# Three edits to the six-layer stage of a one-core transformer kernel: order on TensorE and GpSimd, and a loop written out

## The reference, cut to what matters

```python
q, k, v = split(shift_tokens(x) @ Wqkv)          # 16 heads of 64
q, k = l2norm(q) * qs, l2norm(k) * ksc
q = q * cos * scale + rotate_half(q) * sin * scale
k = k * cos * inv + rotate_half(k) * sin * inv
# windows of 32 tokens, each looks at itself and the one before
attn = softmax(where(mask, -big, q @ k.T * 8.0))
x = (attn @ v) @ Wo + x
x = ffn_layer(shift_tokens(x), ...) + x
```

## Time and profile before

| | |
|---|---|
| median of 3 runs | 2736.19 us (2731.33 to 2745.01) |
| the profiled execution | 2730.72 us |
| its span in the trace | 2728.9 us |
| granted TensorE clock, mean | 0.912 |
| busy: TensorE, VectorE, ScalarE, GpSimd | 2169.6, 1973.4, 1509.5, 1492.2 us |

### The profile page before, as it was taken

How to read it: one execution, slowest core, us unless ns; L and a number is a source line. 1 busy time by engine, 2 the same in 40 slices (tenths; PEclk the granted TensorE clock), 3 DMA queues, 4 the chain that set the end, 5 groups by cost and what they waited for, 6 DMA issues and landing times.

```text
span 2728.9 us, 53797 instructions
## 1 busy us (share of the span) xinstructions
PE 2169.6 (80%) x21684; PEld 1154.6 (42%) x21780; DVE 1973.4 (72%) x2087; ACT 1509.5 (55%) x1863; POOL 1492.2 (55%) x1031
## 2 busy tenths in 40 slices
PE   4768875888998989888889889889988756678734
PEld 1111123555555555555555555555555411111334
DVE  1766628888888888888888888888889426676211
ACT  2255564566676666666766676666766321455600
POOL 5500017777776776777776777777777234100033
PEclk7787897999999999999999999999999866897967
DMA  4100000000001000100010000000000001000133
GB/s 149 60 19 25 13 2 1 17 2 17 2 2 26 17 2 2 26 2 17 1 26 2 17 2 9 19 17 2 1 9 2 1 18 67 22 27 13 32 92 86
DMA packets 55828, 59.08 MB, mean 22 GB/s; under 512 B 13142, under 2 KB 45012, under 8 KB 55508
## 3 DMA queue, kind: packets, MB, share of 16 engines
q1 hardware_dynamic: 53444, 50.77, 6.1%
q0 software_dynamic: 2128, 4.72, 0.7%
HBM read 44.07 MB, written 11.01 MB: 20 GB/s over the span
## 4 chain that ended last, share of the span: by engine, by line
PE 36%; POOL 19%; DVE 17%; issue 16%; ACT 9%; DMA 2%; SPq 1%; POOLq 0%; DVEq 0%; ACTq 0%
PE bank L735 5%; PE bank L706 4%; PE bank L859 4%; DVE big L1463 4%; PE bank L923 4%; PE bank L933 4%; POOL big L580 3%; POOL big L597 3%; POOL big L581 3%; DVE big L1569 3%; POOL small L590 2%; ACT big L1180 2%; ACT pxs L1305 2%; PE bank L976 2%; DVE small L1563 2%
## 5 line engine op out<-in xcount | busy, mean ns | idle before, releaser
L1463 DVE TENSOR_REDUCE big<-bank 128x1 f32<-128x512 f32 x512 | 327.7, 685 | 199.3 <-PE bank L706 195.3
L602 POOL TENSOR_TENSOR sc<-sc,small 128x1024 f32<-128x1024 f32 x96 | 263.4, 2744 | 365.4 <-DVE small L1605 365.4
L859 PE MATMUL bank<-wqk,xs 128*128 128x512 f32 x768 | 359.2, 610 | 13.6 <-ACT xs L1261 8.3
L933 PE MATMUL bank<-pxs,mw 128*128 128x256 f32 x1536 | 366.2, 382 | 0.0
L1296 ACT ACTIVATE sc<-sc 128x1024 f32<-128x1024 f32 x96 | 101.5, 1057 | 464.0 <-DVE sc L1595 463.9
L933 PEld LDWEIGHTS bank<-pxs,mw 128*128 128x128 f32 x1536 | 291.1, 192 | 102.7 <-issue 71.9
L1180 ACT ACTIVATE big<-bank 128x1024 f32<-128x1024 f32 x256 | 250.2, 1026 | 140.1 <-PE bank L720 137.1
L1569 DVE TENSOR_TENSOR big<-big,rotCl 128x2048 f32<-128x2048 f32 x96 | 226.2, 2356 | 78.1 <-POOL big L581 78.1
L706 PE MATMUL bank<-pxs 48*128 48x512 bf16 x512 | 183.6, 439 | 117.1 <-DVE big L1463 74.0
L1563 DVE TENSOR_REDUCE small<-big 128x32 f32<-128x2048 f32 x96 | 219.0, 2281 | 39.5 <-ACT big L1274 30.2
L1584 DVE TENSOR_TENSOR big<-big,small 128x1024 f32<-128x1024 f32 x192 | 246.5, 1284 | 1.1 <-POOL small L592 1.1
(11 more groups left out here) (244 smaller groups left out, 3945.1 us busy)
## 6 DMA issues: line engine op xcount, KB each, us to landing
wqk<-in_L_ffn_Wqkv SPq DMA_DIRECT2D x12, 512.0 KB, 4.4
pxs<-part_rows SPq DMA_DIRECT2D x64, 96.0 KB
pxs<-part_rows SPq DMA_DIRECT2D x64, 64.0 KB
wqk<-in_L_ffn_w SPq DMA_DIRECT2D x16, 256.0 KB, 3.0
wvt<-in_wv_layers_t SPq DMA_DIRECT2D x6, 512.0 KB, 4.7
wol<-in_L_ffn_Wo SPq DMA_DIRECT2D x6, 512.0 KB, 5.8
part_rows<-big SPq DMA_DIRECT2D x24, 128.0 KB
part_rows<-sc SPq DMA_DIRECT2D x24, 128.0 KB
```

The source lines that it names most:

```text
L602: pool.tensor_tensor(p3, p3, rden(i).unsqueeze(2).broadcast_to([P, LH, 64]), ALU.mult).then_inc(l_pn, 1)
L859: m = pe.matmul(bank[:, 2 - 2 * half + c, :], xs[:, b % 2, WIN + i * P:WIN + (i + 1) * P], wqk[:, (2 * half + c) * 512:(2 * half + c + 1) ...
L933: m = pe.matmul(bank[:, 6, part * 2 * P:(part + 1) * 2 * P], mw[:, 2 * (a % 4) + s, a // 4, :], pxs[:, part, a, s, :], start=(a == 0 and s ...
L1463: dve.tensor_reduce(nm[:, qt, 2 * p + r:2 * p + r + 1], bank[:, 4 + r, :], AX.X, ALU.max, negate=True).then_inc(a_mx, 1)
```

## The change

On TensorE, `turn_windows(T)` moves from the end of the slot to the place behind the projections, ahead of the second half of mixing and of `weigh(T - 1)`. Its wait becomes the softmax subtraction of T (`l_e`), since bank 4 holds the scores until then; `weigh` now waits for the eviction of the turned tile (`l_xe`), and the scores for the first eviction of `weighed(T - 2)` (`l_pc`). ScalarE evicts the turned tile right behind the exponentials. GpSimd does the half rotations of T+2 ahead of the division of T. `layer_slots`, and with it the slots of all engines, and SyncE's loop become Python loops, so all rounds stand in the program, with constants to wait on.

```diff
@@ layer_slots
-            with eng.Fori(0, DEPTH - 1) as l:
+            for l in range(DEPTH - 1):
                 for j in range(2, 2 + BATCH):
@@ sync
-            with sp.Fori(1, DEPTH) as l:
+            for l in range(1, DEPTH):
                 load_layer(l, False)
@@ gpsimd slot
-                normalise(T, i)
                 if ahead >= 2:
                     if b == BATCH - 1 and i == 2:
                         pool.wait_ge(l_tab, 3 * l + 6)
                         settle(pool)
                     turn_swapped(T + 2, (i + 2) % TILES)
+                normalise(T, i)
@@ tensor
             def scores(T, it, i):
-                if not (isinstance(T, int) and T == 0):
-                    pe.wait_ge(l_xe, T)
+                if not (isinstance(T, int) and T < 2):
+                    pe.wait_ge(l_pc, 2 * T - 3)
+                elif T == 1:
+                    pe.wait_ge(l_xe, 1)
+                settle(pe)
@@
             def turn_windows(T, b, i):
-                if isinstance(T, int) and T == 0:
-                    pe.wait_ge(l_e, 1)
-                else:
-                    pe.wait_ge(l_pc, 2 * T - 1)
+                pe.wait_ge(l_e, T + 1)
+                settle(pe)
@@ tensor slot
                         project(...)
+                turn_windows(T, b, i)
                 if feeds:
                     feed(fed, fl, i, 2)
                 if mixes:
                     mixing(it, l, b, i, 1)
                 if not (first and i == 0):
                     pe.wait_ge(l_pt, T)
-                    pe.wait_ge(l_e, T + 1)
+                    pe.wait_ge(l_xe, T + 1)
@@
                     weigh(T - 1, i + 3)
                 if feeds:
                     feed(fed, fl, i, 3)
-                turn_windows(T, b, i)
@@ scalar slot
                 exponentials(T, i)
+                windows(T, i)
                 if ahead >= 2:
                     take(T + 2, i % 2, 0)
@@
                         weighed(T - 1, it if i else it - 1, (i - 1) % TILES, half)
-                windows(T, i)
```

## The result

The changed kernel takes 2819.5 us (median of 4 runs, 2811.4 to 2822.3), the one before 2733.8 us in the same comparison: a ratio of 1.0304, 95% interval 1.027 to 1.0338. It is slower, as forecast (2771), but by 86 us instead of 35, and lies above the range (2718 to 2812).

The account below looks back on a forecast made before the run. A ring of waits between GpSimd and VectorE, 17.06 us a turn, with no engine full, was taken as the bound. +46 + 0 - 11 = +35 us on 2730.7 gave 2766, forecast as 2771 for the median; range 2718 to 2812.

Parts of the forecast that it names:

- Part 2: TensorE and ScalarE: tiles of X turned early are not on the ring, counted 0; up to 1 us a slot otherwise.
- Part 3: Rounds written out: the stall at the loop's jumps goes, -11 us, between 0 and -15.
- Part 1: GpSimd's half rotations ahead of the division: +1.9 us an item, +46 us over 24 items, between 0 and +115.
- (a): GpSimd's L580 can start earlier only as ScalarE's eviction L1266 allows: 0.24 us on average.
- (b): VectorE's transpose L1612 now waits for the division, ahead of L1569: up to +1.2 us a slot, +2.7 an item.
- rival B: Something else holds the ring in half of the slots, the transpose stays hidden: Part 1 costs some +15, 2740 us; chance 0.15.
- Rival D: Written out text is fetched too slowly and TensorE stalls in each round; chance below 0.02.
- (1): VectorE: L1569's wait no longer names L581; L1612 waits for L602 instead, about 1 to 2 us a slot.
- (2): GpSimd: L602's mean falls from 2744 towards 1900 ns, L580's rises towards 3.2 us.
- (3): An item takes about 72.2 us; slots after i=2 and i=3 grow by a microsecond, the others hardly change.
- (4): TensorE: the transposes L915 wait for L1595's result, not for L1305.
- (5): No slot of 20.7 us remains at the wraps of the loop.

Follow-up runs that it names:

- both orders: GpSimd's half rotations ahead of the division and X turned early, device loops kept, against the kernel before: 2798.5 us, 1.0233.
- the small-transpose pair: VectorE's L1612 turns 32 of 1024 columns, under GpSimd's new order alone (2695.5 us, 0.9865) and in the kernel before (2702.2 us, 0.9901); ratios to the kernel before.

## Why the prediction was wrong in size

Two steps failed: the term 0 of Part 2, which measures +36 us, and the term -11 of Part 3 taken as the same in company as alone, which measures +19 us on top of both orders. Part 1 was too large by 18 us, which hid some of it.

**Part 1, right in mechanism, too large.** Forecast +46 us, measured +28 (1.0104). The transpose came onto the ring, as steps (a) and (b) had it, and the small-transpose pair shows it: 70 against 32 us. GpSimd's wait moved from L602 to L580 with its size. In this order alone VectorE's waits have

```profile
DVE sc L1612 <- POOL sc L602: 57.3, 30, 2.1
```

so it stands for the division as forecast, though in 30 slots only. The term was mis-sized: +1.9 us an item was forecast, and 28 us over 24 items are 1.2. Items with b=1 of this run take 1.5 us more than before on average, those with b=2 2.0 and with b=3 1.7 (by the starts of their divisions, the last item left out), near the forecast; those with b=0 only 0.1, for there slot i=3 took 18.9 to 20.0 us before and takes about 18 now, so the ring had been held by something else. That is rival B in a quarter of the items (its price was +15). The sum of an ordinary item was better than its parts: in this run slots i=0 and i=1 take 17.9 and 17.8 us against 18.26 and 16.92 before, so the slot after i=3 grew by nothing where +1.2 was forecast, and the one after i=0 by 0.8 where next to nothing was. That they cancel is luck. And "delayed nothing", said of the transpose from one slot, didn't hold for all: it was worth 32 us in the kernel before.

**Part 2, the step that failed.** "I count 0 ... If cover goes, up to 1 us a slot." It measures +36 us (1.013). The sentence before it had the wait ("at most some 2.6 us") and what is queued behind it; measured are 2.0 to 2.3 us in most slots i=2, but about 6 in those of b=3. Two things were missed. The bound for the cost was taken from TensorE's free time as a mean over an item (5.7 us), but the wait falls in one slot of four, just where the largest feed-forward piece is queued, and in the greater part of these slots the clock falls with it (4.44 us for 2.74). And "their users have the 1.2 us more of (b)" covered an order by another edit's loss; alone, it had no such cover, and together the costs added up (1.0233). The other is ScalarE: the projection's eviction was tied to TensorE's transposes, and that had been priced at L1310's 0.39 us, without the wait for its input. Where TensorE is late by itself (the gap in the slot shown above) ScalarE stands 2.51 us for the tile. That is rare in the changed kernel, 11.2 us in 6 slots; it is large only where the transposes stand further back (122.2 us in 75 slots).

**Part 3, right alone, wrong in company.** Forecast -11, measured -14 (0.995) on the kernel before. But the sum took it as a constant, and on top of both orders it is +19 us. Written out text doesn't stall once a round; it stalls inside the scores of some slots for 1.0 to 2.6 us, longer during weight loads. With TensorE's program as before these gaps are no more than in the loop; with the early place they are 21 to 30 us more, and with slack used by the new wait they land on the ring. Rival D ("TensorE stalls in each round ... below 0.02") was nearer to this than its chance, and "against it the 16 slots that are written out already" was a weak argument: the profile of before has such gaps in those slots, which I had not counted. The second lies in the very item of which I said that it "shows no stall":

```profile
546.72 0.33 PE L902 MATMUL bank<-kbuf,qT 64*32 64x64 f32 x12 [1.55 <-issue]
...
2088.05 0.31 PE L902 MATMUL bank<-kbuf,qT 64*32 64x64 f32 x6 [1.95 <-issue]
```

What the Trainium skill ("Runtime: NRT & Kernel Launch", "Instruction fetch mechanics") says of sequential prefetch, that it is hidden, is not what these rows and the packets of q8 show in the scores, which issue 256 instructions (128 weight loads, 128 products) in 1.5 us: the measurement decides. What it says of the jump holds (3.86 us at the wrap).

**The signs listed.** (1) held in part (37.6 us in 20 slots in the changed kernel, not in each); (2) held for L602, but the hold-up is spread over L580 (2587 ns, not 3.2 us) and L581 (2827 ns); (3) held in the sum of an ordinary item (72.98 for 72.2) and not in its slots (+0.8, +0.2, +1.7 and 0.0 us after i=0, 1, 2 and 3), and the items with b=0 and b=1 are mostly 2 to 7 us longer than that; (4) held, and was the cost; (5) held, the wraps are gone, but slots of 20.7 to 24.6 us stand at other places. Of what would make it wrong, the last came true in part: L1591 waits for TensorE's scores, 45.7 us in 33 slots.

**Left open.** Of the 0.012 by which the whole exceeds the sum of its three parts (1.0184), the loads are 0.005. The rest goes with the other gaps, by one trace each. Why the packets come too late in more slots when the tiles are turned early and the rounds written out wasn't tried; a run that moves only the place of TensorE's instructions in the text, with the order kept, would show it.

## What to carry to other kernels

Before moving an instruction on an engine that "has slack", look at the one slot in which its new wait ends last, and at what is queued behind it there; slack as a mean over an item says nothing of that. When a cheap eviction is moved ahead of one that matters, price the wait for its input, not its own duration. And don't add up edits that use the same slack: the same written out rounds go from -14 to +28 us by the order that they are joined with. When an engine stands with no semaphore behind it, look for a packet of the instruction queue that lands just before it goes on.

## What the runs showed of the hardware

TensorE's instructions don't always come in time, in straight text or in a loop: gaps of 1.0 to 2.6 us inside the scores, and up to 5.6 us while weights were loaded (2.3 us at the same place with the loads cut), against 3.7 to 3.9 us for a taken jump in the kernel before. Each such gap of over 1 us, 215 in all traces, ended 1.1 to 1.7 us behind the landing of a 16 KB packet of the instruction queue.

After TensorE had stood 2.0 to 2.3 us for a semaphore in slots i=2, the six matmuls behind took 2.74 us at a granted clock of 1.00 in five of 13 slots and ran slower in eight, up to 4.44 us at 0.62; after 5.9 to 6.1 us they were slower each time (4.03 to 5.33 us). So a short wait in a busy stretch can cost more than itself.
